# Attention inside a pipelined token mixer: softmax maxima folded into the queries, scores made a second time turned, and the summed output in two buffers

## The reference

```python
qkv = (xp @ w_qkv).reshape(B2, N, 3, H, hd).transpose(2, 0, 3, 1, 4)
a = jax.nn.softmax(jnp.einsum('bhnd,bhmd->bhnm', q, k) * scale, axis=-1)
o = jnp.einsum('bhnm,bhmd->bhnd', a, v).transpose(0, 2, 1, 3).reshape(B2, N, C)
o = o @ w_proj + b_proj
```

## Time and profile before

| | us |
|---|---|
| median of 3 runs | 6029.06 |
| lowest, highest | 5992.82, 6056.17 |
| the profiled execution | 6015.9 |
| its span, first to last instruction | 6014.1 |
| DVE busy | 4949.1 |
| PE busy | 4481.5 |
| ACT busy | 3542.3 |
| mean granted TensorE clock | 0.803 of 2.4 GHz |

### The profile page before, as it was taken

How to read it: one execution, slowest core, us unless ns; L and a number is a source line. 1 busy time by engine, 2 the same in 40 slices (tenths; PEclk the granted TensorE clock), 3 DMA queues, 4 the chain that set the end, 5 groups by cost and what they waited for, 6 DMA issues and landing times.

```text
span 6014.1 us, 72139 instructions
## 1 busy us (share of the span) xinstructions
PE 4481.5 (75%) x24044; PEld 2601.8 (43%) x24044; DVE 4949.1 (82%) x3709; ACT 3542.3 (59%) x7970; POOL 1.5 (0%) x9
## 2 busy tenths in 40 slices
PE   4677777777777777777777777777777777777787
PEld 2344444444444444444444444444444444444444
DVE  4988898888889788988988889787888878877871
ACT  2456665556666555666656676565666656655553
POOL 0000000000000000000000000000000000000000
PEclk7788888778788888887888888887888888877775
DMA  5887777777768677776876776766767677665740
GB/s 138 195 184 175 165 163 170 161 165 182 168 150 186 156 157 181 178 163 155 184 169 146 179 177 150 160 152 152 176 148 162 150 165 165 153 157 136 169 101 2
DMA packets 182851, 953.98 MB, mean 159 GB/s; under 512 B 26557, under 2 KB 76157, under 8 KB 84042
## 3 DMA queue, kind: packets, MB, share of 16 engines
q1 hardware_dynamic: 182442, 948.83, 69.0%
HBM read 888.14 MB, written 60.60 MB: 158 GB/s over the span
## 4 chain that ended last, share of the span: by engine, by line
PE 39%; DVE 27%; issue 16%; ACT 10%; DMA 7%; SPq 1%; DVEq 1%; ACTq 0%; POOL 0%; POOLq 0%
DVE hs L1047 11%; DMA out<-h 6%; PE f_ps L658 5%; PE f_ps L647 4%; DVE hs L1036 3%; PE y_ps L470 3%; PE f_ps L546 3%; DVE neg_max L1141 3%; PE f_ps L572 3%; PE f_ps L612 3%; PE a_ps L516 3%; DVE hs L1053 2%; PE f_ps L555 2%; ACT decay L799 2%; PE f_ps L592 2%
## 5 line engine op out<-in xcount | busy, mean ns | idle before, releaser
L1047 DVE TENSOR_TENSOR_SCAN hs<-decay,hs 128x2192 f32<-128x2192 f32 x384 | 1810.7, 4715 | 0.1
L799 ACT ACTIVATE decay<-decay,a_cols 128x273 f32<-128x273 f32 x3072 | 1386.1, 516 | 0.4
L1036 DVE TENSOR_TENSOR hs<-hs,b_ps 128x2192 f32<-128x2192 f32 x384 | 929.7, 2421 | 16.7 <-DMA hs<-dtu_rows 16.7
L1053 DVE TENSOR_TENSOR hs<-hs,c_s 128x2192 f32<-128x2192 f32 x384 | 933.9, 2432 | 10.4 <-issue 10.4
L599 PE MATMUL f_ps<-ident,hid 92*92 92x92 f32 x3456 | 490.1, 291 | 447.7 <-ACT hid L885 447.7
L506 PE MATMUL a_ps<-xn,w_in_s 96*128 96x274 f32 x1536 | 529.0, 474 | 286.0 <-ACT xi L822 186.1
L599 PEld LDWEIGHTS f_ps<-ident,hid 92*92 92x92 f32 x3456 | 360.0, 147 | 635.7 <-ACT hid L885 568.7
L470 PE MATMUL y_ps<-hs,y_pick 128*32 128x274 f32 x6144 | 553.7, 489 | 32.8 <-DVE hs L1053 32.8
L885 ACT ACTIVATE hid<-f_ps,neg_max 92x274 f32<-92x274 f32 x1152 | 463.7, 481 | 170.7 <-DVE neg_max L1141 170.4
L1141 DVE TENSOR_REDUCE neg_max<-f_ps 92x4 f32<-92x1096 f32 x288 | 370.3, 1286 | 226.1 <-PE f_ps L592 226.1
L506 PEld LDWEIGHTS a_ps<-xn,w_in_s 96*128 96x128 f32 x1536 | 321.9, 223 | 475.4 <-ACT xi L822 241.6
(11 more groups left out here) (133 smaller groups left out, 5617.4 us busy)
## 6 DMA issues: line engine op xcount, KB each, us to landing
decay<-dt_rows SPq DMA_DIRECT2D x384, 1096.0 KB, 10.5
hs<-dtu_rows SPq DMA_DIRECT2D x384, 1096.0 KB, 13.9
dt_rows<-dt SPq DMA_DIRECT2D x192, 137.0 KB, 10.4
dtu_rows<-dtu SPq DMA_DIRECT2D x192, 137.0 KB, 10.5
xp<-in_patches SPq DMA_DIRECT2D x32, 588.0 KB, 18.3
out<-h SPq DMA_DIRECT2D x32, 205.5 KB, 11.3
h<-in_txt SPq DMA_DIRECT2D x32, 57.8 KB, 2.3
w_in_s<-in_w_in SPq DMA_DIRECT2D x1, 1152.0 KB
```

The costliest lines, as they stand in the source:

```text
L799: e = act.activation(dec[:, k, t], dec[:, k, t], ACT.Exp, scale=a_cols[:, d * IC + u, TILES * half + k:TILES * half + k + 1])
L1036: dve.tensor_tensor(x[:, :, :], x[:, :, :], b_ps[:, 0:T].unsqueeze(1).broadcast_to([128, TILES, T]), ALU.mult).then_inc(dbu_done, 1)
L1047: dve.tensor_tensor_scan(i, a, i, 0.0, ALU.mult, ALU.add).then_inc(scan_done, 1)
L1053: dve.tensor_tensor(x[:, :, :], x[:, :, :], c_s[d][:, :].unsqueeze(1).broadcast_to([128, TILES, T]), ALU.mult).then_inc(hc_done, 1)
```

## The change

No transposes are left. For each tile of queries the scores are made as before and only their row minima are taken. When a group's three minima are there, `q_with_maxima` makes the group's queries a second time in bank 4, and adds to them by three small products with `ident_4` (four times the identity) the minima, which stand in `neg_max` at row 16 of each head's 32: a padding row, where the queries are zero. `maxima_copy` scales by 1/4 into the place of the old queries. The keys' padding row 16 holds ones (`k_one`, as bias of `k_copy`). `turned_scores` then multiplies keys by queries, tile by tile of keys, which gives the scores turned and with the maximum already taken off; one exponential over four banks (`softmax_exp`) writes `prob_t`. The two kinds of score tiles share banks 0 to 3 in 18 slots, one per gap from 10 to 27, in the order of `SLOTS`. Each group has its own `qk`, two of them in free rows of `hid`. q and k of groups 1 and 2 are made in gaps 11 and 12, the values in gaps 9 and 10, `av` of groups 0 and 1 in gaps 19 and 25. `h2` has two buffers, used in turn.

```diff
-        h2 = sb("h2", [CH, 2, T])
+        h2 = [sb(f"h2_{i}", [CH, 2, T]) for i in range(2)]
...
-        prob = hid[0:QT, 12:16, :]
-        neg_max = sb("neg_max", [QT, 4])
+        qk = [qk_0, hid[:, 12:14, :], hid[:, 14:16, :]]
+        neg_max = sb("neg_max", [QT, 2, 3, 128])
+        ident_4 = sb("ident_4", [QT, QT])
+        k_one = sb("k_one", [128, 1])
...
-        V_GAPS = (10, 11, 12)
+        V_GAPS = (9, 10, 10)
+        Q_GAPS = (11, 12)
         STEPS = 3 * GROUPS
-        SCORE_GAPS = [10 + 2 * s for s in range(STEPS)]
-        TURN_GAPS = [gap + 1 for gap in SCORE_GAPS]
-        Q_GAPS, K_GAPS = (14, 20), (15, 21)
-        AV_GAPS = (16, 22, 28)
-        SUM_GAPS = (17, 23, 28)
-        INV_GAPS = (18, 24, 28)
-        NORM_GAPS = (18, 24, 29)
+        SLOTS = [("s", 0, 0), ("s", 0, 1), ("s", 0, 2), ("s", 1, 0), ("t", 0, 0), ("s", 1, 1), ("t", 0, 1),
+                 ("s", 1, 2), ("t", 0, 2), ("s", 2, 0), ("t", 1, 0), ("s", 2, 1), ("t", 1, 1), ("s", 2, 2),
+                 ("t", 1, 2), ("t", 2, 0), ("t", 2, 1), ("t", 2, 2)]
+        SLOT_GAP = 10
+        MAX_GAPS = (13, 18, 24)
+        AV_GAPS = (19, 25, 28)
+        SUM_GAPS = (20, 26, 28)
+        NORM_GAPS = (21, 27, 29)
...
+            def q_with_maxima(f, g):
+                pe.wait_ge(nmx_done, at(f, STEPS, 3 * g + 3))
...
+                for t in range(3):
+                    new = min(t, 1)
+                    pe.matmul(f_ps[:, 4, QS[t] + new:QS[t] + QT], neg_max[:, g % 2, t, :], ident_4[:, new:QT],
+                              start=True, stop=False, skip_group_check=True)
+                for i in range(2):
+                    mm = pe.matmul(f_ps[:, 4, 0:T], w_qk_s[:, i, 0, g * 128:(g + 1) * 128], cen[:, i, :],
+                                   start=False, stop=(i == 1), skip_group_check=True)
+                mm.then_inc(mx_mm, 1)
...
-            def turn(f, s):
+            def turned_scores(f, g, t):
+                pe.wait_ge(mx_copied, at(f, GROUPS, g + 1))
+                after_slot(f, SLOTS.index(("t", g, t)))
                 for r in range(4):
-                    pe.wait_ge(pexp, at(f, 4 * STEPS, 4 * s + r + 1))
-                    for k in range(3):
-                        mm = pe.transpose(f_ps[0:QT, r, k * QT:(k + 1) * QT],
-                                          prob[:, r, QS[k]:QS[k] + QT], ident[0:QT, 0:QT])
-                    mm.then_inc(pt_mm, 1)
+                    rows = slice(32 * r, 32 * r + 32)
+                    pe.matmul(f_ps[0:QT, r, 0:T], qk[g][rows, 1, QS[t]:QS[t] + QT], qk[g][rows, 0, :],
+                              start=True, stop=True).then_inc(tr_mm, 1)
...
+            def maxima_copy(f, g):
+                act.wait_ge(mx_mm, at(f, GROUPS, g + 1))
+                act.wait_ge(sc_mm, at(f, 4 * STEPS, 12 * g + 12))
+                act.activation(qk[g][:, 0, :], f_ps[:, 4, 0:T], ACT.Copy, scale=HD ** -0.5).then_inc(mx_copied, 1)
...
-            def softmax_exp(f, s):
-                act.wait_ge(nmx_done, at(f, STEPS, s + 1))
-                wait(act, pt_mm, at(f, 4 * STEPS, 4 * s))
-                for r in range(4):
-                    act.activation(prob[:, r, :], f_ps[0:QT, r, 0:T], ACT.Exp, scale=-1.0,
-                                   bias=neg_max[:, r:r + 1]).then_inc(pexp, 1)
-
-            def turn_copy(f, s):
-                g, t = s // 3, s % 3
+            def softmax_exp(f, g, t):
+                act.wait_ge(tr_mm, at(f, 4 * STEPS, 4 * (3 * g + t) + 4))
                 if t == 0:
                     wait(act, av_mm, at(f, GROUPS, g))
-                act.wait_ge(pt_mm, at(f, 4 * STEPS, 4 * s + 4))
-                new = min(t, 1)
-                act.activation(prob_t[:, :, :, QS[t] + new:QS[t] + QT],
-                               f_ps[0:QT, 0:4, 0:3 * QT].rearrange("p r (k t) -> p r k t", k=3)[:, :, :, new:],
-                               ACT.Copy).then_inc(pt_copied, 1)
+                act.activation(prob_t[:, :, t, :], f_ps[0:QT, 0:4, 0:T], ACT.Exp).then_inc(pexp, 1)
...
-                wait(dve, out_stored, at(f, 16, 0))
+                wait(dve, out_stored, at(ago(f, 1), 16, 0))
```

More of the change, by code:

```diff
@@ L677, in fine_early @@
                     qk_mm_one(f, 0, 1, 1)
[L678 to L685, removed]
+                if gap in Q_GAPS:
+                    qk_mm_one(f, Q_GAPS.index(gap) + 1, 0, 4)
+                if gap == V_GAPS[1]:
+                    v_mms(f, 1)
+                if gap in AV_GAPS:
+                    av(f, AV_GAPS.index(gap))
+                if gap in SUM_GAPS[:2]:
+                    spread_sums(f, SUM_GAPS.index(gap))
                 if gap == PROJ_GAP:
@@ L689, in fine_late @@
             def fine_late(f, small, gap):
-                if gap in V_GAPS:
-                    v_mms(f, V_GAPS.index(gap))
-                if gap in Q_GAPS:
[L693 to L697, removed]
+                if gap == V_GAPS[0]:
+                    v_mms(f, 0)
+                if 0 <= gap - SLOT_GAP < len(SLOTS):
+                    kind, g, t = SLOTS[gap - SLOT_GAP]
+                    if kind == "s":
+                        scores(f, g, t)
+                    else:
+                        turned_scores(f, g, t)
+                if gap == V_GAPS[2]:
+                    v_mms(f, 2)
+                if gap in Q_GAPS:
+                    qk_mm_one(f, Q_GAPS.index(gap) + 1, 1, 4)
+                if gap in MAX_GAPS:
+                    q_with_maxima(f, MAX_GAPS.index(gap))
+                if gap == SUM_GAPS[2]:
+                    spread_sums(f, 2)
                 if gap in FC1_GAPS:
@@ L932, in fine_mid @@
                         rstd(f_ps[0:CH, 2, 0:T], rstd_f, f_var, at(f, 3, j + 1), f_ln, at(f, 4, 2 * j if j else 1), f_rstd)
[L933 to L940, removed]
+                if gap == V_GAPS[1]:
+                    v_copy(f, 1)
+                if gap in Q_GAPS:
+                    q_copy(f, Q_GAPS.index(gap) + 1, 4)
+                if gap in AV_GAPS:
+                    av_copy(f, AV_GAPS.index(gap))
+                if gap in SUM_GAPS[:2]:
+                    invert_sums(f, SUM_GAPS.index(gap))
             def fine_late(f, small, gap):
@@ L948, in fine_late @@
                     k_copy(f, 0, 1)
-                if gap in Q_GAPS:
[L950 to L957, removed]
+                    v_copy(f, 0)
+                if 0 <= gap - SLOT_GAP < len(SLOTS):
+                    kind, g, t = SLOTS[gap - SLOT_GAP]
+                    if kind == "t":
+                        softmax_exp(f, g, t)
+                if gap == V_GAPS[2]:
+                    v_copy(f, 2)
+                if gap in Q_GAPS:
+                    k_copy(f, Q_GAPS.index(gap) + 1, 4)
+                if gap in MAX_GAPS:
+                    maxima_copy(f, MAX_GAPS.index(gap))
+                if gap == SUM_GAPS[2]:
                     invert_sums(f, 2)
@@ L1133, in add_mixer, with row_maxima @@
                 for i in range(2):
-                    a = dve.tensor_scalar(h2[:, i, :], h2[:, i, :], feat_s[:, i, P_LNB:P_LNB + 1], None, ALU.add)
+                    a = dve.tensor_scalar(h2[parity(f)][:, i, :], h2[parity(f)][:, i, :], feat_s[:, i, P_LNB:P_LNB + 1], None, ALU.add)
                 a.then_inc(h2_ready, 1)
[L1137 to L1141, removed]
+            def row_maxima(f, g, t):
+                dve.wait_ge(sc_mm, at(f, 4 * STEPS, 4 * (3 * g + t) + 4))
+                wait(dve, mx_mm, at(f, GROUPS, 1 if g == 2 else 0))
+                dve.tensor_reduce(neg_max[:, g % 2, t, :].rearrange("p (r c) -> p r c", r=4)[:, :, HD],
+                                  f_ps[0:QT, 0:4, 0:T], AX_X, ALU.min).then_inc(nmx_done, 1)
             def divide_sums(f, g):
@@ L1311, in front @@
                             .then_inc(s_c, 1)
-                dve.wait_ge(s_c, 32)
+                dve.wait_ge(s_c, 35)
                 for i in range(2):
```

66 lines of the change are left out of this document (41 added, 25 removed).

## The result

| us | before | after |
|---|---|---|
| median, 4 runs each, same chip | 6031.27 | 6240.53 |
| lowest to highest | 5992.82 to 6056.17 | 6226.78 to 6249.29 |
| profiled execution | 6015.9 | 6226.8 |
| its span | 6014.1 | 6225.0 |
| mean granted TensorE clock | 0.803 | 0.781 |

The changed kernel is slower, by a ratio of 1.0351 (1.0292 to 1.0409). The forecast was 6054 us, with a range of 5940 to 6150; the time lies above the range.

What follows compares the result with a forecast made beforehand. No engine was full, so waits of DVE, the busiest at 82%, were taken to decide. New waits of 279 us less 253 removed gave +26, with the last item +25: 6054 us from a median of 6029.06, range 5940 to 6150.

Steps and rivals of the forecast that it cites:

- The store: DVE's wait for the output store: two `h2` buffers remove all 83.6 us, 2.7 us per item.
- Work removed and added: Engine busy time: PE 490 us out, 485 in, so unchanged; ACT 426 us less, counted as no gain.
- Gap 10, the new wait: First scores behind value product, `x_proj` and sum: DVE waits 6.0 us per item instead of 0.71 (4.9 to 8.5).
- Gaps 11 to 17: Second and third maxima together wait 0 to 2.4 us, taken as 1.0; from gap 13 on none waits.
- Gap 19: Scores after group 1's last maximum: wait 0.2 us at the upper clock, 5.3 at the lower, taken as 2.0.
- Sum: New waits of 9.0 us per item, 279 us over 31 items, less 253 removed: +26 (-95 to +249).
- Last item: The item running alone at the end: 77.9 us before, 77 after (67 to 87), so -1 (-11 to +9).
- Two readings: Middle item's timeline: four maxima wait for nothing; clock rows: both levels occur within one item.
- the loss went behind the attention: Sign to look for: a grown wait before the inverted sums or the roots; no size given.
- a cold burst at gap 19: Slower rival: PE enters gap 18 at the lower clock, new waits 11 to 16 us per item, 6116 to 6271; chance 0.18.
- PE at the upper clock: Faster rival: upper clock from gap 9 to 19, new waits 5.1 to 7.7 us per item, 5933 to 6014; chance 0.28.
- The other two: Rivals: store's wait returns as another, 6138, chance 0.06; maxima cease to wait, all 253 us gone, 5775, chance 0.06.

Runs made afterwards that it cites:

- third experiment: The changed kernel with 16 unread products per item added on PE where it idles, order otherwise unchanged: 6082.03 us, 1.0105 to the kernel before.
- fifth experiment: The changed kernel with gap 25's turned scores ahead of group 1's `av`, and `x_proj` ahead of the last `av`: 6080.82 us, 1.0092 to the kernel before.
- first: The changed kernel with gap 10's first scores ahead of the value product, `x_proj` and the sum of states: 6152.88 us, 1.0225 to the kernel before.
- fourth: The kernel before with two buffers of `h2` and nothing else: 5912.01 us, 0.9831 to the kernel before.
- sixth experiment: The changed kernel with scores first in gaps 10, 11, 19, 25, `x_proj` ahead of the last `av`, and unread products: 5920.27 us, 0.9838 to the kernel before.
- second: The changed kernel with gap 19's scores ahead of `av` and the sum of states: 6188.57 us, 1.0299 to the kernel before.

## Why the prediction was wrong

- **The store** was right: 83.6 us of waits gone, nothing in their place at that point. Alone it brought 102.
- **Work removed and added.** ACT's sum was right but for 70 us: 3184 against about 3120; the 288 wide exponentials took 311.2 us, as forecast. PE's is 4535, 54 above the 4481 of before and just outside the 50 allowed, and this near miss is made of larger ones. What came in took 594 us, not 485: the turned scores 291.5 for 265, the second queries 170.9 for 147, the small products 131.3 for 73. `av`, the same work as before, went from 208 to 285 us, as nearly all of it now ran at the lower clock. The rest of PE's list took 127 us less.
- **Gap 10, the new wait** was right in kind and place, and 1.3 us too large: 4.7 in the mean against 6.0. The term that was off is `x_proj` at the lower clock. At 1.60 us in place of 2.98 the same sum gives 4.6. The step took the clock of one item's row; 6 of the 31 items of the same trace had the other one.
- **Gaps 11 to 17.** Forecast 1.0 for both of the doubtful minima, measured 0. From gap 13 on none waits, as said.
- **Gap 19** was right in mechanism and mis-sized: 5.2 us per item against 2.0, which is the upper end that the step gave for the lower clock (5.3). The step had no row that spoke for a value between its ends, and took one. The third experiment shows that with this order the clock decides: 0 or 7.3 us by the same instructions.
- **Sum.** The three terms measure 9.9 us per item (307.8 over 31 items) against 9.0. The small miss of this sum hides larger ones that cancel: +3.2 at gap 19, -1.3 at gap 10, -1.0 at gaps 11 to 17. With 9.9 in place of 9.0 the forecast would have been 6083, inside its range.
- **Last item**: from its first minimum's wait to its last inverted sums it takes 80.6 us, where 78.6 were measured before and 77 (67 to 87) was forecast. Its minima wait 47.5 us instead of 56.8, its inverted sums 20.5 instead of 9.5.
- **Two readings** of the rows were wrong and changed no number. In the earlier trace rows there are nine minima, so that six of them wait for nothing, not four. And the earlier trace rows show only the lower clock; it is the earlier trace rows that have both levels within one item.
- **What was left out.** The step that failed is the one that was never taken. The list of changed places ended at gap 19; the forecast named the wait before the inverted sums only among the signs to look for ("the loss went behind the attention") and let its 113.0 us stand. It grew by 161 us, 150 of it in the 31 items and 11 in the last, more than the forecast missed the range by (6240.53 - 6150 = 91). The working for it would have been that of gaps 10 and 19 once more: in the new order the last `av` stands behind two more turns of turned scores and exponential, and ACT's silu with its two table loads, which cost nothing there before, now holds up the first of them. The fifth experiment removes 132 of these 161 us without touching the minima.

Of the rivals, *a cold burst at gap 19* came nearest. Its mechanism is what the trace shows, and its range of 6116 to 6271 holds the time; but only half for its reason: gap 19 was at its upper end, gap 10 below its lower one (4.9), and the missing part came from the end of the attention. The Trainium skill (TensorE: Matmul & The Clock Gate, part 1), which the forecast names with it, says that activity releases the throttled clock. An estimate by that rule, with gap 19 at its upper end, was about 6155; gap 19 did go that way. *PE at the upper clock* came true at gap 10 alone. The other two did not come about: the store's 83.6 us were cashed, and the minima wait longer than before.

Put together: minima and store give 129 - 84 = +45, the inverted sums +161, the roots +23, and all others 6 - 22 = -16, in all 213, within 2 us of the 211 measured. Why the roots wait 23 us longer remains open: they are at 149 to 151 in the first, fourth and sixth experiment, below the 161 of before, yet at 194 in the second.

## What to carry to other kernels

Where a change re-times a whole chain, walk the chain to its last consumer, and cost every wait that it releases, above all the one whose releaser is not in the diff. Where two ends of a term are two clocks of PE, one row does not tell which it will be: look at the same place in all items, and cost both. In a kernel that PE does not bound, taking work off PE can cost time: in the middle item shown, the bursts behind 3.03, 5.60 and 6.18 us of idle PE all ran at the lower clock, and unread products in the idle time made the kernel faster. And an instruction whose operands are long there should not stand behind one whose operand comes late: moving `x_proj` ahead of the last `av` brought 1.0% in the old kernel, while the new attention was slower than the old one with one buffer, with two, and with each in its best order of those tried.

## What the runs showed of the hardware

The granted clock of one place in the program is not fixed, even within one execution: in the third experiment the same gaps 18 and 19 were at 1.00 in one item and at 0.50 in the next, strictly alternating over eight items near the end, and one such switch was worth 7.2 us. In the kernel before, `x_proj` in gap 10 was at the upper level in 6 of 31 items. What selects the one or the other was not settled. Unread products on idle PE brought 1.0351 / 1.0105 = 1.024, some 150 us, though the kernel with them has 1024 more matmul records to run. `av` took 1.56 to 1.60 us at the upper clock and 2.97 at the lower. Of its 96 calls in a launch, 40 ran wholly at the upper level before the change and none after it.
